# Selective scan with merged channel halves, separate B and C row loads, and paused gathers

## What is computed

```python
def step(h, inp):
    dt_t, u_t, B_t, C_t = inp
    dA = jnp.exp(dt_t[..., None] * A)
    h = dA * h + (dt_t * u_t)[..., None] * B_t[:, None, :]
    y_t = jnp.einsum('bds,bs->bd', h, C_t)
    return (h, y_t)
```

## Time and profile before

| quantity | value |
|---|---|
| median of 3 runs | 585.29 us |
| the profiled execution | 589.76 us |
| its span, first to last instruction | 588.4 us |
| PE busy | 480.0 us (82%) |
| DVE busy | 407.8 us (69%) |
| ACT busy | 314.7 us (53%) |
| POOL busy | 319.8 us (54%) |
| mean granted TensorE clock | 0.916 |

### The profile page before, as it was taken

The page is one execution under the profiler, slowest core; times in us unless marked ns, Lnnn a source line. Parts: engine busy times, 40 slices in busy tenths (PEclk is TensorE's granted clock), DMA queues, the critical chain, the costliest instruction groups (busy, mean ns, idle before and its releaser), DMA issues.

```text
span 588.4 us, 7447 instructions
## 1 busy us (share of the span) xinstructions
PE 480.0 (82%) x2128; PEld 276.2 (47%) x2128; DVE 407.8 (69%) x821; ACT 314.7 (53%) x655; POOL 319.8 (54%) x298
## 2 busy tenths in 40 slices
PE   3987878988789984899788997887778677899936
PEld 1744446565459951363233443333324233489614
DVE  4588692974453333299999799999997997544303
ACT  2573656454435530557665885978386641646200
POOL 1059541553452172046789669897989666411450
PEclk9898996997898996989997998999798899899976
DMA  8999920000033410154555354566465630043321
GB/s 299 410 324 326 319 78 0 2 20 18 19 103 110 122 49 22 43 146 140 160 156 143 111 154 114 163 144 184 112 168 138 161 109 20 19 113 112 85 60 53
DMA packets 39991, 73.94 MB, mean 126 GB/s; under 512 B 4368, under 2 KB 20240, under 8 KB 39184
## 3 DMA queue, kind: packets, MB, share of 16 engines
q1 hardware_dynamic: 35600, 67.00, 38.0%
q0 software_dynamic: 2048, 4.20, 2.5%
q10 hardware_dynamic: 2304, 2.29, 1.2%
HBM read 66.00 MB, written 26.28 MB: 157 GB/s over the span
## 4 chain that ended last, share of the span: by engine, by line
PE 33%; DVE 24%; issue 15%; ACT 12%; POOL 8%; another core or an unknown queue 5%; DMA 2%; SPq 1%; DVEq 0%; POOLq 0%; ACTq 0%
DVE arena L1313 9%; PE psum L699 5%; PE psum L751 5%; POOL arena L1904 4%; PE psum L881 3%; PE psum L712 3%; PE psum L763 2%; PE psum L800 2%; DVE psum L1307 2%; ACT L1391 2%; ACT arena L1712 2%; ACT xn L1421 2%; PE psum L457 1%; POOL by_expert L1821 1%
## 5 line engine op out<-in xcount | busy, mean ns | idle before, releaser
L1904 POOL TENSOR_TENSOR arena<-arena 128x512 f32<-128x512 f32 x127 | 158.3, 1271 | 68.0 <-DVE arena L1313 67.7
L881 PE MATMUL psum<-arena,w 128*128 128x512 f32 x256 | 136.4, 652 | 27.8 <-POOL arena L1904 25.8
L1313 DVE TENSOR_TENSOR_SCAN arena<-arena,psum 128x512 f32<-128x512 f32 x128 | 148.4, 1200 | 8.3 <-ACT arena L1712 4.8
L1712 ACT ACTIVATE arena<-arena 128x510 f32<-128x510 f32 x128 | 87.2, 713 | 41.9 <-DVE arena L1313 39.5
L881 PEld LDWEIGHTS psum<-arena,w 128*128 128x128 f32 x256 | 46.6, 201 | 102.8 <-POOL arena L1904 76.4
L1307 DVE TENSOR_TENSOR psum<-psum,arena 128x512 f32<-128x512 f32 x128 | 81.5, 681 | 1.1 <-DMA arena<-bc_store 1.0
L699 PE MATMUL psum<-xnt,w 128*128 128x512 f32 x128 | 64.2, 651 | 10.2 <-ACT arena L1554 10.2
L1789 POOL TENSOR_TENSOR arena<-arena 128x512 f32<-128x512 f32 x16 | 20.7, 1295 | 69.6 <-DVE arena L1014 69.6
L1858 POOL DMA_INDIRECT arena<-by_expert,routes x32 | 30.6, 956 | 29.8 <-DMA by_expert<-arena 20.6
L699 PEld LDWEIGHTS psum<-xnt,w 128*128 128x128 f32 x128 | 25.5, 208 | 39.4 <-issue 27.5
L1821 POOL DMA_INDIRECT by_expert<-xn,routes x32 | 33.7, 1053 | 14.3 <-issue 7.9
(11 more groups left out here) (199 smaller groups left out, 826.8 us busy)
## 6 DMA issues: line engine op xcount, KB each, us to landing
arena<-bc_store SPq DMA_DIRECT2D x64, 512.0 KB, 4.9
by_expert<-w_in SPq DMA_DIRECT2D x4, 4096.0 KB, 43.4
w<-w_in SPq DMA_DIRECT2D x1, 4427.5 KB, 13.4
by_expert<-arena SPq DMA_DIRECT2D x56, 64.0 KB, 1.6
arena<-by_expert SPq DMA_DIRECT2D x54, 64.0 KB, 2.0
by_expert<-w_in SPq DMA_DIRECT2D x1, 1984.0 KB, 66.8
x<-x_in SPq DMA_DIRECT2D x4, 256.0 KB, 7.5
out<-x SPq DMA_DIRECT2D x4, 256.0 KB
```

The lines of the kernel that those rows point to most:

```text
L881: nc.tensor.matmul(bank(6 + c), ident, state[c][s % 3], start=False, stop=(n == DS - 1)).then_inc(*summed.inc((s, c)))
L1313: nc.vector.tensor_tensor_scan(state[c][s % 3], decay_b[c][s % 2], bank(2 + c), 0.0, ALU.mult, ALU.add).then_inc(*state_ready.inc((s, c)))
L1712: nc.scalar.activation(live, seq, ACT.Exp, scale=a_neg[:, DS * c + n:DS * c + n + 1]).then_inc(*decay_ready.inc((s, c)))
L1904: nc.gpsimd.tensor_tensor(state[c][s % 3], state[c][s % 3], bc_row[s % len(bc_row)][:, 1, :], ALU.mult).then_inc(*y_done.inc((s, c)))
```

## The change

- DVE does one product and one scan of 128x1024 in a step, over both halves, instead of two of each of 128x512. Step 0 keeps both split, and the last step keeps its scans split.
- The product of step s + 1 stands ahead of the scan of step s. Its result goes in turn into three buffers, `drives`: PSUM banks 0 and 1, a new SBUF piece, PSUM banks 2 and 3.
- The product reads `dtu` from SBUF and the row of B from SBUF, broadcast over the halves. The copy of `dt*u` to PSUM (`entered`, L1717) goes.
- There are three decay buffers instead of two and four state buffers instead of three; ACT prepares the decay two steps ahead. `state_ready` and `driven` are signalled once in a step.
- B and C rows have four buffers each and their own DMAs of 256 KB; B is loaded two steps ahead and its buffer is free when the product is done, C's when `y_done` is.
- In the tables, group 1's dt is projected and its softplus done two to three steps earlier, and `ready_sp` is two steps later for groups 1 to 3.
- The gathers: in turn 0 POOL waits before every group for the landings of the one before; in turn 1 it waits once, before group 2, for those of group 1.

```diff
-        decay_b = [[piece(BANK) for _ in range(2)] for _ in range(NCH)]
-        state = [[piece(BANK) for _ in range(3)] for _ in range(NCH)]
-        bc_row = [piece(2 * BANK).rearrange("p (k t) -> p k t", k=2) for _ in range(4)]
+        decay_b = [piece(NCH * BANK) for _ in range(3)]
+        state = [piece(NCH * BANK) for _ in range(4)]
+        b_row, c_row = ([piece(BANK) for _ in range(4)] for _ in range(2))
+        drives = [psum[:, 0:2, :].rearrange("p b t -> p (b t)"), piece(NCH * BANK), psum[:, 2:4, :].rearrange("p b t -> p (b t)")]
...
-        ready_pool = {13: 1, 27: 2, 43: 3}
-        ready_sp = {0: 0, 10: 1, 24: 2, 40: 3}
+        ready_pool = {11: 1, 27: 2, 43: 3}
+        ready_sp = {0: 0, 12: 1, 26: 2, 42: 3}
...
-                    nc.vector.tensor_tensor(bank(c), dt_b[:, c, group(0)], u[:, c, group(0)], ALU.mult).then_inc(*first_drive.inc(c))
+                    nc.vector.tensor_tensor(dtu[:, c, group(0)], dt_b[:, c, group(0)], u[:, c, group(0)], ALU.mult).then_inc(*first_drive.inc(c))
...
+                def drive(s):
+                    g, n = steps[s]
+                    i, to = s % len(b_row), drives[s % len(drives)]
+                    dve.wait_ge(*b_loaded[i][s])
...
+                    if s >= len(drives):
+                        dve.wait_ge(*state_ready[s - len(drives), NCH - 1])
+                    nc.vector.tensor_tensor(to.rearrange("p (c t) -> p c t", c=NCH), dtu[:, :, group(g)],
+                                            b_row[i].unsqueeze(1).to_broadcast([P, NCH, BANK]), ALU.mult).then_inc(*driven.inc((s, NCH - 1)))
...
-                        nc.vector.tensor_tensor(bank(2 + c), bank(c), bc_row[i][:, 0, :], ALU.mult).then_inc(*driven.inc((s, c)))
...
+                    dve.wait_ge(*driven[s, NCH - 1])
+                    dve.wait_ge(*decay_ready[s, NCH - 1])
+                    if s >= len(state):
+                        dve.wait_ge(*summed[s - len(state), NCH - 1])
+                    nc.vector.tensor_tensor_scan(to, decays, entering, 0.0, ALU.mult, ALU.add).then_inc(*state_ready.inc((s, NCH - 1)))
...
+                drive(0)
                 for s in range(n_steps + 1):
+                    if s + 1 < n_steps:
+                        drive(s + 1)
                     if s < n_steps:
                         recur(s)
...
-                    if g >= 2:
-                        pool.wait_ge(*read_back[g - 2][t, GB * (g - 1) - 1])
+                    if g == 2 or (g and t == 0):
+                        pool.wait_ge(*read_back[g - 1][t, GB * g - 1])
...
-                        nc.gpsimd.tensor_tensor(state[c][s % 3], state[c][s % 3], bc_row[s % len(bc_row)][:, 1, :], ALU.mult).then_inc(*y_done.inc((s, c)))
+                        y = half(state[s % len(state)], c)
+                        pool.wait_ge(*state_of(s, c))
+                        pool.wait_ge(*c_loaded[s % len(c_row)][s])
+                        nc.gpsimd.tensor_tensor(y, y, c_row[s % len(c_row)], ALU.mult).then_inc(*y_done.inc((s, c)))
```

More of the change, by code:

```diff
@@ L415, in build, with state_of @@
         both = [(s, c) for s in step_events for c in range(NCH)]
-        driven, state_ready, summed = (signal(n, both) for n in ("driven", "state_ready", "summed"))
+        last = n_steps - 1
+        split_drive, split_state = (0,), (0, last)
+        driven = signal("driven", [(s, c) for s, c in both if s in split_drive or c == NCH - 1])
+        state_ready = signal("state_ready", [(s, c) for s, c in both if s in split_state or c == NCH - 1])
+        summed = signal("summed", both)
+        def state_of(s, c):
+            return state_ready[s, c if s in split_state else NCH - 1]
         y_done, y_last = signal("y_done", both[:-1]), signal("y_last", [0])
@@ L433, in build @@
         exit_a = [output_done[n_units - 1], gated[BATCH - 1], squared[BATCH - 1], rotated_ready[rotations[-1]]]
-        last = n_steps - 1
         exit_b = [summed[last, NCH - 1], gated_last[NCH - 1], y_last[0]]
@@ L880, in add_up @@
                         pe.wait_ge(*(y_last[0] if (s, c) == both[-1] else y_done[s, c]))
-                        nc.tensor.matmul(bank(6 + c), ident, state[c][s % 3], start=False, stop=(n == DS - 1)).then_inc(*summed.inc((s, c)))
+                        nc.tensor.matmul(bank(6 + c), ident, half(state[s % len(state)], c), start=False, stop=(n == DS - 1)).then_inc(*summed.inc((s, c)))
                 def project_out(g, ring):
@@ L897, in project_out @@
                     r.then_inc(*out_b_made.inc(g))
-                rings = [Ring([bank(i + c) for c in range(NCH)], [mark[last, c] for c in range(NCH)]) for i, mark in ((0, driven), (2, state_ready))]
+                rings = [Ring([bank(0), bank(1)], [state_ready[last, c] for c in range(NCH)]),
+                         Ring([bank(2), bank(3)], [state_ready[last - 1, NCH - 1]] * NCH)]
                 for s in range(n_steps + 1):
@@ L1278, in enter_scan @@
                 for c in range(NCH):
-                    for i in range(2):
-                        starts = decay_b[c][i].rearrange("p (s t) -> p s t", t=SEQ)[:, :, 0:1]
+                    for decays in decay_b:
+                        starts = half(decays, c).rearrange("p (s t) -> p s t", t=SEQ)[:, :, 0:1]
                         r = nc.vector.memset(starts, 0.0)
@@ new lines, in recur @@
+                def recur(s):
+                    to, decays, entering = state[s % len(state)], decay_b[s % len(decay_b)], drives[s % len(drives)]
+                    if s in split_state:
+                        for c in range(NCH):
+                            dve.wait_ge(*driven[s, c if s in split_drive else NCH - 1])
+                            dve.wait_ge(*decay_ready[s, c])
+                            if s >= len(state):
+                                dve.wait_ge(*summed[s - len(state), c])
+                            nc.vector.tensor_tensor_scan(half(to, c), half(decays, c), half(entering, c), 0.0,
+                                                         ALU.mult, ALU.add).then_inc(*state_ready.inc((s, c)))
+                        return
+                    dve.wait_ge(*driven[s, NCH - 1])
+                    dve.wait_ge(*decay_ready[s, NCH - 1])
+                    if s >= len(state):
+                        dve.wait_ge(*summed[s - len(state), NCH - 1])
+                    nc.vector.tensor_tensor_scan(to, decays, entering, 0.0, ALU.mult, ALU.add).then_inc(*state_ready.inc((s, NCH - 1)))
@@ L1712, in prepare @@
                         nc.scalar.activation(live, seq, ACT.Exp, scale=a_neg[:, DS * c + n:DS * c + n + 1]).then_inc(*decay_ready.inc((s, c)))
-                    if n == 0 and g >= 1:
-                        act.wait_ge(*dtu_ready[g])
-                        for c in range(NCH):
-                            act.wait_ge(*driven[s - 1, c])
-                            nc.scalar.activation(bank(c), dtu[:, c, group(g)], ACT.Copy).then_inc(*entered.inc((g, c)))
-                for s in range(-1, n_steps + 1):
-                    if s + 1 < n_steps:
-                        prepare(s + 1)
+                for s in range(-2, n_steps + 1):
+                    if s + 2 < n_steps:
+                        prepare(s + 2)
                     for what, g in due_in_steps(s):
@@ L1933, in spread_rows, with load_b @@
             def spread_rows():
-                for s, (g, n) in enumerate(steps):
+                def load_b(s):
+                    g, n = steps[s]
+                    i = s % len(b_row)
                     if s in ready_sp:
```

73 lines of the change are left out of this document (40 added, 33 removed).

## The result

The changed kernel takes 628.91 us (median of 6 runs, 622.88 to 629.96), the kernel before beside it 584.74 us (median of 6). The ratio is 1.074 [1.067, 1.082]: slower, by 44 us. The forecast was 633. A ratio is taken over a part of the runs, without the slow ones, so it can differ a little from the quotient of the two medians beside it.

What follows compares the result with a forecast made beforehand. DVE bounds the scan before; after the change POOL would, at 4.6 us a step. Median 585.3 + 60 (stage) - 12 (gathers) = 633 us, own range 620 to 645 (chance 0.45); 590 to 660 holds 0.8.

Steps and rivals of the forecast that it cites:

- main term: Scan stage: POOL's SBUF reads stand while DVE streams two SBUF inputs; the stage grows by 60 us.
- POOL's part: POOL in the scan: own work 159 + 35, blocks by DVE 104, less 5, so 293 us instead of 234.5.
- DVE in turn lost little: DVE in the scan: reading beside POOL costs it little; L1335 took 745 ns where L1171 has 684.
- The 5 us taken off for the sends: POOL in the scan: some blocks fall where it doesn't read (descriptors in sends, waits at group starts), 5 us off.
- The 60 us of idle time: Sign in the scan: DVE idles before its scans for POOL's product by way of PE's addition, over 60 us.
- +18 us on my sum: Scan: by the skill's rule of full waits, the sum goes toward the upper bound, some 18 us above.
- DVE's own instructions: DVE in the scan: merged product 1.21 us, scan 2.24 long; a step 3.27 us, 0.15 less, 9 us over 62.
- The gathers: Gather runs: pauses release waiting engines earlier, gaining 5 us in turn 0 and 7 in turn 1, 12 in all.
- No block: Rival, scan: POOL reads between DVE's reads and DVE stays the bound; 565 us, chance 0.20.
- Half a block, only products: Rival, scan: only DVE's products stop POOL, not its scans; 42 us off POOL's time, 597 us, chance 0.08.
- Pauses of no use: Rival, gathers: freeze ends with the last gather, POOL blocked; 650 us, chance 0.27 shared with DVE waits' upper bound.
- Hidden parts: Scan: ACT's decays, PE's additions, B and C loads, SP's order, moved dt and softplus add nothing.

Runs made afterwards that it cites:

- both experiments on them: Kernel before with only the gathers' waits changed: 563.05 us against 586.16; changed kernel with the old gather waits: 652.05 us, ratio 1.104.

## Why the prediction came out as it did

**Direction and main term: right.** The stage was to grow by 60 us and grew by 62; POOL's own stretch (first product to end of last) was to be 293 us and was 541.5 - 245.6 = 295.9, 4.6 us a step as forecast (over steps with nothing else on POOL, 4.1). The mechanism is the one named: POOL's reads stand while DVE reads two inputs from SBUF. The merged kernel with PSUM inputs and the one without C products are the two controls, and both lose the cost.

**The size of POOL's part: right as a sum, shared out otherwise.** The C product's mean was to be near 2.1 us and was 1.83, so the blocks on it cost (1827 - 1271) ns x 127 = 71 us. The rest of the 104 fell elsewhere: L1920 and L1917 went from 2353 to 3538 and 3338 ns, and the gates (L1945) from 1264 to 1756, L1841 from a median of 1042 to a mean of 2024, the sends (L1851) from 1004 to 1364; with their counts 3.6 + 3.0 + 3.0 + 2.9 + 3.6 = 16 us. So the blocks came to 87 us, against 104 - 5 = 99. Another 12.3 us POOL idled for DVE's scan, which the sum didn't have at all; that the two make up 99 again is luck. The 5 us taken off for the sends were wrong in kind: these stand too, by 0.36 us each. Over steps with nothing else on POOL 2.1 us a product was exact: 21.18 us for ten.

**"DVE in turn lost little": wrong.** This step rested on one pair of rows where DVE came second and lost 61 ns. The pair was misread: L1335 began at 490.77 and POOL's product ended at 490.97, so there were only 0.2 us left to wait for. A wait in full until 0.13 us before that end, the offset found for POOL, would be 0.07 us; the rows could not tell a small loss from a full one. In the changed kernel DVE's products are 42 x (1.99 - 1.21) + 21 x (1.48 - 1.21) = 38 us longer than planned (12.7 of it in a single one, see the last section) and its scans from SBUF 21 x (3.24 - 2.27) = 20 us. The 60 us of idle time that DVE was to show before its scans were 10.8, of them 7.4 for PE, since the time went into the instructions. That did little harm to the total, since by the forecast DVE had those 60 us to lose; that the error stayed without effect was luck. With POOL less loaded the same error would have shown: in the kernel with all products in PSUM, DVE stands 1.1 us in a step, and my expectation there missed by 44 us, in the main for the same reason. The rule of the Trainium skill, "SBUF — State Buffer", section "Who interferes with whom", which I had weighed and set below that one pair of rows, says that the second comer waits in full; the trace of that kernel agrees (1.1 us behind a product of 1.27). One instance at the very end of a stage was too thin to outweigh it. Its price was not the +18 us on my sum either: the stretch is 3 us above the 293. That price let each of DVE's instructions with two SBUF inputs wait for a whole product, and in the cycle shown two of four do (1.1 and 1.0 us), the other two 0.1.

**DVE's own instructions: right.** 1.20 and 2.27 us where nothing collides, 3.32 us a step without C products against 3.27. That the merge saves about 0.1 us a step is so only if the product stands a step ahead, and in this layout of PSUM that went with inputs in SBUF, which cost ten times what it saves (62 us of the stage against 64 x 0.1).

**The gathers: right in direction, mis-sized, the release not seen.** Where I took 5 and 7 us, the changed kernel has 12.0 and 10.5, and the pauses alone 12 and 12. I assumed that the freeze sets in, a pause ends it, and part of the gain is lost again in the next burst. In turn 0 nothing freezes at all, with four in a row or with eight; in turn 1 what is left ends 1.6 us after the last gather, not at the pause.

**The rivals.** No block: refuted by the 1827 ns. Half a block, only products: refuted by POOL's product of 3.25 us under a scan and by the scan rows, 3237 against 2275 ns. Pauses of no use: refuted by both experiments on them. The balance against the profiled execution: +62.5 instead of +60 in the stage, -22.5 instead of -12 around it, 629.8 instead of 637.8; between the medians the forecast is 4 us high.

**Hidden parts: right but for ACT.** The loads of B and C and SP's order don't show: DVE has no idle time for B rows in the scan, and POOL's idle time before its C products is for DVE alone. ACT shows a little: 3.4 of the 10.8 us before DVE's scans are for its decay, in spite of the third buffer.

## What to carry to other kernels

Where GpSimd reads SBUF beside VectorE, give VectorE's two-input instructions one input in PSUM; here merging was worth 0.1 us a step, and a collision of two readers cost about 1 us. Read the lengths of the same form of instruction in two places (here 2275 and 3237 ns) before the idle times: a wait inside an instruction shows nowhere else. And when idle time after a run of indirect gathers is put down to nothing on the core, try a wait for their landings between them: each left GpSimd idle for 1.9 us in place of 0.3, and the gain was 17 to 23 us in three sets of runs. In a fourth set the kernel before ran as fast without them, so measure both.

## What the runs showed that I had not expected

VectorE doesn't always get its turn between GpSimd's instructions. In the cycle shown further up the two take turns: the product at 316.12 waits for one product of GpSimd, and the next of GpSimd waits for it. But once in the changed kernel a product of VectorE waited behind ten of them:

```profile
406.95 13.87 DVE L1327 TENSOR_TENSOR psum<-arena 128x1024 f32<-128x1024 f32 x1
```

```profile
407.46 4.93 POOL L1935 TENSOR_TENSOR arena<-arena 128x512 f32<-128x512 f32 x4
...
417.24 2.48 POOL L1935 TENSOR_TENSOR arena<-arena 128x512 f32<-128x512 f32 x2
```

13.87 us for an instruction of 1.20, while POOL's ten ran at their undisturbed 1.23 each; DVE ended only after POOL had run out of work at 419.72. The kernel without pauses has such a case too, of 12.19 us, and the one with all products in PSUM two, of 9.44 and 9.45. What decides between the two behaviours is open.

The freeze remains unexplained. During a run of 16 gathers DVE and ACT don't go on with PE's results, and both start again within 0.1 us of each other, about 3 us after the last one. In runs of four no such idle time showed, in runs of eight none in turn 0 and, in seven profiles, 4.2 to 4.6 us in turn 1, there 1.6 us after the last. In one set of runs, of 17, the kernel before took 563.27 us, what it takes with pauses elsewhere; it was not profiled there, so that the freeze was absent is only likely. What speaks for it: the three kernels that were profiled in that set also have eights in turn 1, and none of them has the 4 us. The same chip gave 585.62 in a later set. What decides it is open.
